# Two-layer decoder on one core: new instruction orders for all engines, layer-0 norms as phases, expert weights in two parts

## The reference

```python
x = x + _L0_attn_ref(_layernorm(x), ...)      # delta rule: 4 heads of 32, a recurrence over 64 tokens
x = x + _L0_xattn_ref(_layernorm(x), ctx, ctx, ...)   # causal cross attention, 16 heads of 8
x = x + _L0_ffn_ref(_layernorm(x), ...)       # 6 layers: local attention, 16 heads of 64, rotary; gated Gelu FFN
x = x + _L1_attn_ref(_layernorm(x), ...)      # causal attention, 16 heads of 8, normed q and k, scores clipped
x = x + _L1_xattn_ref(_layernorm(x), ctx, ctx, ...)   # gated linear attention, 8 heads of 16
x = x + _L1_ffn_ref(_layernorm(x), ...)       # 16 experts 128 -> 256 -> 128, the top 3 weighted
```

```python
for i in range(6):
    x = attn_layer(shift_tokens(x), Wqkv[i], q_scale[i], k_scale[i], Wo[i]) + x
    x = ffn_layer(shift_tokens(x), ln_g[i], ln_b[i], W1[i], b1[i], W2[i], b2[i]) + x
```

## Time and profile before

| | |
|---|---|
| median of 3 runs | 4436.27 us (4430.77 to 4455.68) |
| profiled execution, its span | 4433.1 us |
| PE busy | 4137.5 us, 93% |
| PE weight loads | 3049.0 us, 69% |
| DVE busy | 3566.6 us, 80% |
| ACT busy | 3444.4 us, 78% |
| POOL busy | 2650.6 us, 60% |
| granted TensorE clock, mean | 0.969 of full speed |

### The profile page before, as it was taken

How to read it: one execution, slowest core, us unless ns; L and a number is a source line. 1 busy time by engine, 2 the same in 40 slices (tenths; PEclk the granted TensorE clock), 3 DMA queues, 4 the chain that set the end, 5 groups by cost and what they waited for, 6 DMA issues and landing times.

```text
span 4433.1 us, 150676 instructions
## 1 busy us (share of the span) xinstructions
PE 4137.5 (93%) x61520; PEld 3049.0 (69%) x61520; DVE 3566.6 (80%) x11101; ACT 3444.4 (78%) x9647; POOL 2650.6 (60%) x2210
## 2 busy tenths in 40 slices
PE   7999989999999999999999999999999689999999
PEld 5777756666666666666666666666666478888888
DVE  4666599999889888899898989898989357766775
ACT  3555478889888888888888988888888357776776
POOL 3444377777777777777777777777777133333331
PEclk8888899999999999999999999999999789999999
DMA  3000000000000000000000000000000100000000
GB/s 101 4 4 4 4 3 4 5 3 4 29 4 4 4 28 4 4 4 13 20 3 4 5 28 4 4 4 8 7 9 9 47 2 4 4 4 4 4 4 6
DMA packets 65258, 46.43 MB, mean 10 GB/s; under 512 B 29220, under 2 KB 63032, under 8 KB 63800
## 3 DMA queue, kind: packets, MB, share of 16 engines
q1 hardware_dynamic: 64568, 36.78, 2.9%
HBM read 28.48 MB, written 2.10 MB: 7 GB/s over the span
## 4 chain that ended last, share of the span: by engine, by line
PE 68%; ACT 13%; DVE 10%; POOL 5%; issue 5%; SPq 0%; DVEq 0%; DMA 0%; ACTq 0%; POOLq 0%
PE ps L557 56%; PE ps L561 12%; ACT BIG L909 7%; DVE BIG L1109 5%; POOL BIG L1549 5%; ACT L909 2%; ACT BIG L901 2%; DVE sm L1120 2%; ACT ps L901 1%; DVE BIG L1117 1%; DVE BIG L1114 1%; POOL sm L1552 0%; DVE sm L1117 0%; DVE BIG L1187 0%; DVE sm L1113 0%
## 5 line engine op out<-in xcount | busy, mean ns | idle before, releaser
L557 PE MATMUL ps<-WB,BIG 128*128 128x128 f32 (+2 forms) x8576 | 1941.9, 363 | 8.4 <-ACT BIG L901 3.4
L901 ACT ACTIVATE BIG<-ps 128x512 f32<-128x512 f32 (+6 forms) x3168 | 1484.0, 530 | 538.8 <-PE ps L561 407.7
L1549 POOL TENSOR_TENSOR BIG<-BIG,sm 128x512 f32<-128x512 f32 (+1 forms) x864 | 1219.0, 1426 | 788.7 <-DVE sm L1319 473.5
L557 PEld LDWEIGHTS ps<-WB,BIG 128*128 128x128 f32 (+1 forms) x8576 | 1142.2, 193 | 217.6 <-issue 175.6
L561 PEld LDWEIGHTS ps<-t_ident,BIG 128*128 128x128 f32 x6016 | 705.8, 144 | 541.4 <-issue 250.2
L561 PE MATMUL ps<-t_ident,BIG 128*128 128x128 f32 x6016 | 916.2, 282 | 162.5 <-ACT BIG L901 53.3
L1549 POOL TENSOR_TENSOR BIG<-BIG 128x512 f32<-128x512 f32 x768 | 967.2, 1280 | 144.1 <-DVE BIG L1109 144.1
L1120 DVE TENSOR_REDUCE sm<-BIG 128x8 f32<-128x512 f32 (+3 forms) x1472 | 882.6, 611 | 174.5 <-ACT BIG L909 172.2
L557 PEld LDWEIGHTS ps<-BIG 64*64 64x64 f32 (+2 forms) x37888 | 626.0, 130 | 364.6 <-issue 93.1
L557 PE MATMUL ps<-BIG 64*64 64x64 f32 (+4 forms) x37888 | 774.7, 225 | 69.7 <-ACT BIG L901 18.7
L909 ACT ACTIVATE BIG<-ps 128x512 f32<-128x512 f32 (+1 forms) x832 | 512.1, 616 | 257.3 <-PE ps L557 252.3
(11 more groups left out here) (120 smaller groups left out, 2985.1 us busy)
## 6 DMA issues: line engine op xcount, KB each, us to landing
WB<-in_Wqkv SPq DMA_DIRECT2D x6, 1536.0 KB, 7.4
XS<-y_sb SPq DMA_DIRECT2D x96, 63.0 KB
y_sb<-in_ctx SPq DMA_DIRECT2D x16, 256.0 KB, 3.1
WB<-in_Wo SPq DMA_DIRECT2D x6, 512.0 KB, 9.1
x_sb<-in_x SPq DMA_DIRECT2D x8, 256.0 KB, 5.0
WB<-in_F_W SPq DMA_DIRECT2D x1, 2048.0 KB, 8.6
WB<-in_F_W SPq DMA_DIRECT2D x8, 256.0 KB, 6.5
out<-x_sb SPq DMA_DIRECT2D x8, 256.0 KB, 2.3
```

The source lines that it names most:

```text
L557: return te.matmul(o, l, r, start=start, stop=stop, skip_group_check=not check)
L901: return se.activation(o, i, ACT.Copy)
L1549: return pe_.tensor_tensor(o, a, b, op)
```

## The change

The orders of all four engines are written anew for all three stages. The lags of C are larger by about four slots (PE's `o` from 6 to 9, `x` from 0 to 4), since the norms of layer 0 are now phases of their tiles (`d1 d2 d3` and `d4` on DVE, `d` on POOL) at lags 0 to 2. One function, `schedule`, gives each engine its whole list, sorted by a due time made of a begin for each stage and engine, a slot length and the place in the string; the begins lie far enough apart that no instruction of a stage comes ahead of one of the stage before on its engine. The PSUM banks are handed out over the whole list, so banks are carried over from stage to stage. The waits for a whole stage are replaced by waits for the tiles whose buffers or banks are taken over. C has 12 rings of semaphores instead of 8. The expert weights go out in two parts: the first matrices after the third shift of the last layer, the second after the last attention output product. After the last Gelu, ACT loads a set that holds both Exp and Ln.

Of the strings two lines of each side stand here:

```diff
 C_ORDER = {
-    "act": "1b04 1q02 1a04 1b14 2g04 2g14 2g24 1f04 1f14 1a14 1q12 1v04 2sh2 1p05 1o06 1o16 1x1 1k02 1s04 1k12 "
-           "2tr3 1s14 1v13 1p15",
+    "act": "1s18 1v17 1q05 1a07 1b07 1b17 2g07 1f07 1q15 2g27 1a17 1f17 2tr6 2sh5 2g17 1k05 1v07 1o09 1o19 1x4 1p18 "
+           "1k15 1p08 1s07",
...
-    "pool": "1first1 1n13 1q12 1k02 1q02 1p04 1k12 2sh2 1p14 1n02",
+    "pool": "1k17 1d2 1n07 1n17 2sh6 1q06 1k06 1p08 1q16 1p18",
...
+SLOT = {"ab": 13.5, "c": 11.5, "de": 25.2}
+BEGIN = {
+    "ab": {"pe": 4.7, "act": -27.6, "dve": -18.2, "pool": -15.0},
+    "c": {"pe": 1020.5, "act": 1004.6, "dve": 1017.1, "pool": 998.8},
+    "de": {"pe": 4720.8, "act": 4678.2, "dve": 4700.7, "pool": 4710.1},
+}
...
-        CC = ring_units(kinds, "c", 8)
+        CC = ring_units(kinds, "c", 12)
...
-        def all_ab():
-
-            return [u.on("dve", "y") for u in AB[-8:]]
-
-        def all_c():
-            return all_ab() + [u.on("dve", "x") for u in uC2.values() if u.at["l"] == depth - 1]
+        def after_one(u):
+
+            return [AB[29 + 2 * u.at["t"]].on("pe", "w")] if AB and u.at["l"] == 0 and u.at["t"] < 2 else []
+
+        def after_two(u):
+
+            if not AB or u.at["l"] or u.at["t"] > 2:
+                return []
+            return [[AB[31].on("pe", "w"), AB[30].on("pe", "y")], [AB[30].on("pe", "y"), AB[31].on("pe", "y")], [AB[31].on("pe", "y")]][u.at["t"]]
...
+        def schedule(e):
+
+            due = []
+            for seq, order, stage in ((AB, AB_ORDER, "ab"), (CC, C_ORDER, "c"), (DE, DE_ORDER, "de")):
+                items = [(o[:-1], int(o[-1])) for o in order[e].split()]
+                for n in range(len(seq) + 10):
+                    for j, (ph, lag) in enumerate(items):
+                        u = unit(seq, n - lag)
+                        if u and stage == "c" and (u.kind[1] != ph[0] or ph[1:] in NORM and u.at["l"]):
+                            continue
+                        if u:
+                            due.append((BEGIN[stage][e] + SLOT[stage] * (n + j / len(items)), u, ph[1:] if stage == "c" else ph))
+            return [d[1:] for d in sorted(due, key=lambda d: d[0])]
...
+        def take(u, ph, marks, wide, banks):
+
+            nonlocal turn
+            turn += turn % wide
+            u.bank[ph], u.after[ph] = turn % banks, ()
+            for i in range(wide):
+                u.after[ph] += full[(turn + i) % banks]
+                full[(turn + i) % banks] = tuple((u, *m.split()) for m in marks)
+            turn += wide
...
+                        if g == 2 and l == depth - 1 and "F" in stages:
+                            expert_weights_1()
+                if "F" in stages:
+                    for s in qkv_free(depth - 1):
+                        w.wait_ge(*s)
+                    expert_weights_2()
                 for i in (6, 7) if "E" in stages else ():
                     context(i)
-                for s in qkv_free(depth - 1) + [uC2[(depth - 1, 7)].on("pe", "o")]:
-                    w.wait_ge(*s)
...
                 if ph == "x":
                     w.wait_ge("const", 3)
+                    if l + t == 0:
+                        prime(0)
+                        prime(1)
...
-                for s in all_c() if t == 0 else []:
-                    w.wait_ge(*s)
...
                     o = act(b.hT[0:m, 512 * n:512 * n + 512], K[0:m, :], ACT.Gelu, bias=T["b1"][0:m, 6 * l + 3 + n:6 * l + 4 + n])
+                    if u is last2 and ph == LAST_GELU:
+                        o.then_inc(u.name("act", ph, sems), 1)
+                        se.preload_act_table_set("natural_log_exp_and_others")
+                        return
...
+                if ph in NORM:
+                    p = t % 4
+                    if ph == "d1":
+                        w.wait_ge(*c1_x(t, "C"))
+                        w.wait_ge(f"c{t // 4}", 16)
+                        o = ve.bn_stats(st0[:, p, :], x_sb[:, t, :])
+                    elif ph == "d2":
+                        w.wait_ge(*u.on("dve", "d1"))
+                        o = ve.bn_aggr(mv0[:, p, :], st0[:, p, :])
+                    elif ph == "d3":
+                        w.wait_ge(*u.on("dve", "d2"))
+                        o = ts(sm_[p][:, 0, 16:17], mv0[:, p, 1:2], 1e-5, None, ALU.add)
+                    else:
+                        w.wait_ge(*u.on("pool", "d"))
+                        o = ts(y_sb[:, t, :], x_sb[:, t, :], mv0[:, p, 0:1], sm_[p][:, 0, 17:18], ALU.subtract, ALU.mult)
```

More of the change, by code:

```diff
@@ L107 @@
 C_ORDER = {
[7 rows of a table removed]
[7 rows of a table added]
 }
-SILENT = ("first", "second")
+NORM = ("d1", "d2", "d3", "d", "d4")
 for _kind in "12":
@@ L160, in __init__ @@
         self.base = dict(base)
-        self.marks = MARKS["C2f" if at.get("last") else kind]
+        self.marks = MARKS[kind + "f" if at.get("last") or at.get("l") == 0 and kind == "C1" else kind]
         self.count = dict.fromkeys(ENG, 0)
@@ L408, in build @@
+        full, turn, primed = [()] * 8, 0, [(), ()]
+        for u in AB + CC + DE:
             if u:
                 u.bank, u.after = {}, {}
[L410 to L426 removed]
+        def take(u, ph, marks, wide, banks):
[6 more added lines that the diff above has]
+            turn += wide
@@ new lines, in build @@
+        order = schedule("pe")
+        places = [i for i, (u, ph) in enumerate(order) if u.stage == "c"]
+        for i, (u, ph) in enumerate(order):
+            banks = 6 if places and places[0] <= i <= places[-1] else 8
+            if places and i == places[0]:
+                primed = [full[6], full[7]]
+            u.after[ph] = ()
+            if u.stage == "ab":
+                if ph in AB_EMPTIED:
+                    take(u, ph, AB_EMPTIED[ph], 1 + (ph in AB_PAIRS), banks)
+            elif u.stage == "de":
+                if ph in DE_EMPTIED:
+                    take(u, ph, DE_EMPTIED[ph], 1 + (ph in DE_PAIRS), banks)
+            elif u.kind == "C1" and ph == "s":
+                u.bank.update({"s0": 6, "s1": 7})
+                full[6], full[7] = ((u, "act", "s0"),), ((u, "act", "s1"),)
+            elif u.kind == "C1" and ph == "y":
+                for h in "01":
+                    take(u, "y" + h, ("act o" + h,), 1, 6)
+                u.after["y"] = u.after["y0"] + u.after["y1"]
+            elif u.kind == "C2" or ph != "w":
+                take(u, ph, EMPTIED[u.kind[1] + ph], 1, 6)
@@ L701, in half, with prime @@
                 return slice(64 * (par ^ hf), 64 * (par ^ hf) + 64)
+            def prime(h):
+                w.wait_ge("k_a", 16 * len(SETS["a"]))
+                for v, e, m in primed[h]:
+                    w.wait_ge(*v.on(e, m))
+                for i in range(4):
+                    o = mm(bank[6 + h][:, 128 * i:128 * i + 128], ident[:, :], ident[:, :], start=(i == 0), stop=(i == 3))
+                o.then_inc(sems["prime"], 1)
             def pe_c1(u, ph):
@@ L967, in act_c1 @@
                     w.wait_ge(*u.on("pe", "x"))
-                    if four:
-                        w.wait_ge(*four.on("pe", "v0"))
-                        w.wait_ge(*four.on("pe", "v1"))
+                    for m in ("q0", "q1", "k0", "k1", "v0", "v1") if four else ():
+                        w.wait_ge(*four.on("pe", m))
                     copy(c_xT(u)[0:64, :], K[0:64, 0:128])
```

197 lines of the change are left out of this document (74 added, 123 removed), and 36 rows, old and new, of tables (AB_ORDER, C_ORDER, DE_ORDER).

## The result

The changed kernel takes **4668.79 us** (median of 4 runs, 4667.12 to 4670.39) against 4440.59 us of the kernel before, run beside it (4 runs, 4430.77 to 4455.68): a ratio of **1.0505, 95% interval 1.0484 to 1.0527**. The prediction said 4324 us, with a range of 4235 to 4425. The change was to be faster by 112 us, and is slower by 228: the sign is wrong.

What follows compares the result with a forecast made beforehand. PE was taken as the bound everywhere, so a new order returns only its waits: -45 - 6 - 46 - 7 - 1 - 7 = -112, span 4321, plus 3.2 gives 4324 us; range 4235 to 4425.

Steps and rivals of the forecast that it cites:

- C, the steady cycle: Stage C's repeating cycle: 1.0 us of PE's waiting goes per cycle, 46 cycles, -46 us (-86 to +40).
- a second limit: Stage C: DVE, busy 54 us of the 60.3 us cycle, also limits; the gain was taken as 1.0 per cycle.
- rival A: All stages: PE is fully fed, every wait in C, DE and AB goes; -175, 4261 us; chance 0.24.
- Rival D: Stage C: slower, ACT's `v1` too late in every attention slot, PE's `a1` waits; +163, 4533 us; chance 0.12.
- C, filling: First five slots of stage C: 13.6 us each falls to about 12.2 with the new POOL order; -7 us.
- DE: -51 expected: Stage DE: two PE stalls shrink in 28 slots, -45 us; table loads leave filling and drain slots, -6.
- PE's wait of 0.88 for ACT: DE slot: PE's stall behind a 1.28 us table load on ACT goes whole, -0.88 us per slot.
- the wait before `ct` of 0.30: DE slot: six expert groups instead of four shrink PE's 1.20 us stall for DVE by 0.90, to 0.30.
- AB: -7 and +-20 for the clock: Stage AB: half of 0.46 us waiting per tile goes, 32 tiles, -7; clock effect taken as nothing, +-20 in range.
- Seams, expert weights: Stage changes: single-buffer waits replace whole-stage waits, -1 us; expert weights loaded earlier, nothing, or 1 us if the shift is held up.

Runs made afterwards that it cites:

- r_after: Changed kernel, order untouched, with the nine small Newton operations of each C tile made one-input TENSOR_REDUCE, inverse roots left out: 4401.35 us (0.9890).
- the control: Kernel before with its nine Newton operations per C tile made one-input TENSOR_REDUCE, inverse roots left out: 4414.91 us (0.9932).
- b_pre: Kernel before with one line added, ScalarE loading the Exp and Ln set once behind stage C's last Gelu: 4439.50 us (0.9986).
- a_de: Changed kernel with only stage DE's table of order put back to that of the kernel before: 4655.66 us (1.0462).
- a_all: Changed kernel with all three tables of order (AB, C, DE) put back, its other parts kept: 4446.93 us (1.0005).

## Why the prediction was wrong

**C, the steady cycle, is the step that failed: -46 expected, +168 measured.** It was costed from the order of the steps with the durations of the kernel before; "What ACT must do ... is unchanged in amount" was right, and was silently extended to DVE. The text names DVE as "a second limit", busy 54 us of 60.3, and then asks only when its work falls, not how long it gets. Its small steps were short because POOL stood idle beside most of them: their 0.19 us was a property of the place. r_after shows both halves. The distances followed were right: PE is fully fed at 57.9 us, rival A's state, and stage C gains 98 us on the kernel before, 66 on the control. The duration of nine operations a tile, and of `ep`, turned that into a loss of 168.

The Trainium skill, page "SBUF — State Buffer", section "Who interferes with whom", has the rule: a DVE instruction with two inputs in SBUF contends with a GpSimd instruction that reads SBUF, and so does a `tensor_scalar` in its 2-port mode. The two engines share one port pair, which the one that issues first holds for its whole instruction, while the other is blocked. A `tensor_reduce`, or an operation with at most one SBUF input outside those modes, doesn't contend. This trace agrees: 192 to 579 ns for two inputs, 672 for 668 in the reduction, 175 for the replacement. For `ep` (170 to 1112) it agrees if `ep` runs in the 2-port mode, which no run shows. The prediction did not use this page. From its rows alone the term has only a wide bound: 37 operations a cycle, each by up to one POOL operation of 1.24, or 46 us; 10 were measured.

**Rival D had the sign and nothing else.** PE's longest waits in C are for DVE's rotations, not for ACT's `v1`, and 4533 falls short by 136 us (the rival counts 48 cycles, the forecast 46; with 46 it is 4526). No rival had an operation that gets longer.

**C, filling: -7.** The first slots repeat every 13.3 us (POOL's scaling at 624.77 and 638.10), not 12.2; 13.6 before. The term is nearly nothing: 0.3 us in each of five slots.

**DE: -51 expected, +10 measured.** The steps as such came true in part: no load in DE, PE's wait of 0.88 for ACT gone with it in b_pre. What failed is the premise that a wait taken from PE is time gained, since the prediction left the clock of DE at 1.00. In b_pre it is worth 25 us by that wait (28 times 0.88) and -1 by the stage. The new order's own part is a loss of 8 (965.4 against 957.8 in a_de): instead of the wait before `ct` of 0.30, an expert group waits 1.28 for a bank that DVE frees. A full-clock slot is so 26.62, not the 25.1 to 25.9 of the forecast, and most slots are not at the full clock.

**AB: -7 and +-20 for the clock, +55 measured.** The old order starts C between 549 and 567 us in nine kernels' profiles, the new one between 597 and 608 in five. So 55 is about 44 by the means, and the scatter of one run. Single slots of before and after, from the window of each:

```profile
140.47:154.50 14.03, 13.56 (x477) 10.64 (x477) 9.98 (x39) 7.79 (x28) 7.14 (x8) 1.00 0.02 4
154.50:171.09 16.59, 16.13 (x477) 12.39 (x477) 10.04 (x39) 8.11 (x28) 7.17 (x8) 0.79 0.01 4
```

```profile
236.10:251.03 14.93, 13.82 (x478) 10.73 (x477) 10.67 (x38) 7.76 (x28) 7.03 (x7) 1.00 0.02 3
251.03:270.04 19.01, 18.79 (x477) 14.31 (x476) 10.88 (x38) 8.69 (x30) 7.06 (x7) 0.64 0.02 4
```

The full-clock slot is 0.9 us longer, and the slot with a part at the low level by 2.4, with more of it at that level (0.64 for 0.79). Over 25 slots before (91.17 to 478.34) and 26 after (77.20 to 519.57) the mean is 15.5 and 17.0 us; PE is busy 15.0 and 15.9 of it. So of 1.5 us a slot 0.87 come from PE's work running slower and 0.65 from waiting: the waits that were to shrink have grown from 0.46 to 1.11 us. "No row tells me which way the new order tips it" was honest, but +-20 was too narrow for a stage in which about every second slot is at a mixed clock. Which part of the AB order lengthens the low stretches, and what the 19.6 us without a releaser are, stays open.

**Seams, expert weights: -1 and nothing.** Right as far as a_all can tell (1.0005; it can't resolve 1 us).

## What to carry to other kernels

Before moving an operation, read its mean in rows that keep shapes apart, and ask what the neighbour engine does meanwhile: here a DVE operation with two SBUF inputs was short beside an idle GpSimd (0.18 us) and beside a busy one lasted until GpSimd's own ended (up to 1.24), and the profile counts the waiting as busy. To test it, leave the order and change the operation's kind; moving it changes both. A wait taken from TensorE isn't time gained until a run has shown the granted clock beside it: in stage C of r_after the clock stayed at 1.00 and the time came, in DE of b_pre it went from 1.00 to 0.95 and took the time back.
